# One register load for a group's expert weights, and key, turn, routing and ranks one or two slots later, in a sine-attention and mixture-of-experts kernel

## What is computed

```python
h = layernorm(x)
Q, K, V = (proj(h, W, b) for W, b in ((Wq, bq), (Wk, bk), (Wv, bv)))   # 16 heads of 8
attn = sin(30.0 * einsum('bhqd,bhkd->bhqk', Q, K) / sqrt(8))
x = x + einsum('bsd,ed->bse', heads_joined(einsum('bhqk,bhkd->bhqd', attn, V)), Wo) + bo

h = layernorm(x)
probs = sigmoid(einsum('bsh,eh->bse', h, Wr) + rb)                     # 8 experts
scores, idx = top_k(probs, 2)
cw = (one_hot(idx, 8) * scores[..., None]).sum(-2)
expert(h, Wg, Wu, Wd) = silu(h @ Wg.T) * (h @ Wu.T) @ Wd.T             # 128 -> 256 -> 128
x = x + expert(h, *shared) + sum_e cw[..., e:e+1] * expert(h, *routed[e])
```

## Time and profile before

| | |
|---|---|
| runs | 492.1, 491.87, 494.67 us; median 492.1 |
| profiled execution | 491.92 us, its span 490.0 us |
| mean granted TensorE clock | 0.981 |
| busy in the span | TensorE 427.6 us (87%), ScalarE 340.5 (70%), VectorE 292.0 (60%), GpSimd 238.6 (49%) |

### The profile page before, as it was taken

One profiled execution on the slowest core, in us unless ns is written; L12 is line 12 of the kernel. 1 busy time (PEld: TensorE's weight loads), 2 busy tenths in 40 slices (PEclk: granted clock), 3 DMA queues, 4 the chain that ended last, 5 costly groups with the idle time before them and its releaser, 6 DMA issues.

```text
span 490.0 us, 12316 instructions
## 1 busy us (share of the span) xinstructions
PE 427.6 (87%) x4432; PEld 224.0 (46%) x4432; DVE 292.0 (60%) x999; ACT 340.5 (70%) x470; POOL 238.6 (49%) x308
## 2 busy tenths in 40 slices
PE   2898899999978999899999998999999787978771
PEld 1321233323322445444554444444445776967761
DVE  6876685554723446578574666754654544547783
ACT  1668889878869986788688876777876453654540
POOL 5332450300565243228686854256856845567631
PEclk9999999999999999999999999999999978999996
DMA  5047589456046424962465349911122434431111
GB/s 166 2 132 207 117 245 328 91 159 166 18 128 178 98 56 123 185 121 70 132 189 127 70 135 191 167 55 55 50 61 56 104 98 111 113 98 44 50 50 32
DMA packets 82186, 56.05 MB, mean 114 GB/s; under 512 B 28752, under 2 KB 76496, under 8 KB 82128
## 3 DMA queue, kind: packets, MB, share of 16 engines
q1 hardware_dynamic: 77824, 47.74, 38.5%
q0 software_dynamic: 3584, 7.35, 5.6%
q10 hardware_dynamic: 720, 0.20, 0.2%
HBM read 22.62 MB, written 27.13 MB: 102 GB/s over the span
## 4 chain that ended last, share of the span: by engine, by line
PE 55%; issue 12%; DVE 11%; ACT 9%; another core or an unknown queue 3%; POOL 3%; DMA 3%; SPq 1%; ACTq 0%; DVEq 0%; POOLq 0%
PE o_ps L713 15%; PE score L700 8%; ACT attn L975 6%; PE tile_ps L840 4%; PE tile_ps L838 3%; PE tile_ps L839 3%; PE tile_ps L863 2%; DVE hid L1308 2%; ACT gate L996 2%; PE score L840 2%; DMA y_back<-in_wd 2%; PE r_ps L682 1%; PE score L838 1%; PE r_ps L669 1%
## 5 line engine op out<-in xcount | busy, mean ns | idle before, releaser
L975 ACT ACTIVATE attn<-score 128x1024 f32<-128x1024 f32 x256 | 248.5, 1025 | 31.3 <-PE score L700 26.2
L1532 POOL TENSOR_TENSOR hid_lo<-hid,hid_hi 128x256 f16<-128x256 f32 (+1 forms) x94 | 72.4, 771 | 157.8 <-DVE hid_hi L1316 125.2
L713 PE MATMUL o_ps<-attn,vals 128*32 128x512 f32 x1024 | 136.4, 604 | 0.8 <-ACT o_t L982 0.5
L700 PE MATMUL score<-queries,keys 64*128 64x512 f16 x512 | 83.3, 383 | 11.1 <-ACT attn L975 7.7
L1308 DVE SCALAR_TENSOR_TENSOR hid<-tile_ps,gate 128x256 f32<-128x256 f32 (+1 forms) x88 | 40.3, 458 | 55.6 <-ACT gate L996 44.7
L996 ACT ACTIVATE gate<-tile_ps 128x256 f32<-128x256 f32 (+1 forms) x88 | 36.4, 414 | 44.3 <-PE tile_ps L840 35.9
L838 PE MATMUL tile_ps<-xt,w_hi 128*128 128x128 f16 x244 | 43.9, 219 | 1.3 <-ACT y_sb L1008 0.7
L839 PE MATMUL tile_ps<-xt,w_hi 128*128 128x128 f16 x244 | 43.9, 219 | 0.8 <-issue 0.8
L840 PE MATMUL tile_ps<-xt,w_lo 128*128 128x128 f16 x244 | 43.9, 219 | 0.5 <-issue 0.5
L700 PEld LDWEIGHTS score<-queries,keys 64*128 64x128 f16 x512 | 18.5, 93 | 55.8 <-ACT attn L975 31.8
L863 PEld LDWEIGHTS tile_ps<-w_hi,hid_hi 128*128 128x128 f16 x152 | 14.7, 97 | 58.9 <-issue 53.2
(11 more groups left out here) (223 smaller groups left out, 993.6 us busy)
## 6 DMA issues: line engine op xcount, KB each, us to landing
q_four<-q_parts SPq DMA_DIRECT2D x14, 256.0 KB
queries<-q_four SPq DMA_DIRECT2D x14, 256.0 KB
k_four<-k_minus SPq DMA_DIRECT2D x14, 256.0 KB
keys<-k_four SPq DMA_DIRECT2D x14, 256.0 KB
y_sorted<-y_sb SPq DMA_DIRECT2D x52, 64.0 KB
x_sorted<-zeros SPq DMA_DIRECT2D x2, 1472.0 KB, 8.9
queries<-q_three SPq DMA_DIRECT2D x14, 192.0 KB
keys<-k_three SPq DMA_DIRECT2D x14, 192.0 KB
```

What stands on the lines that cost most here:

```text
L700: mm = pe.matmul(score[h][:, i, :], keys[b % 2][rows, 2 * j + h, kt * P:(kt + 1) * P], queries[b % 2][rows, 2 * j + h, :], start=True, sto ...
L713: mm = pe.matmul(o_ps[32 * i:32 * i + 32, :], vals[b % 2][:, kt, h:h + 32], attn[k % RING][:, i, :], start=(k == 0), stop=(k == UNITS - 1))
L975: act.activation(attn[k % RING][:, 2 * (u % 2):2 * (u % 2) + 2, :], score[u % 2][:, :, :], ACT.Sin, scale=SIN_SCALE).then_inc(sined, 1)
L1532: pool.tensor_tensor(cells(hid_lo, d), cells(hid, d), cells(hid_hi, d), ALU.subtract).then_inc(lo_by_pool, 1)
```

## The change

The planner's batch goes from 6 to 23, so each group has one look-up with all its offsets. They come at slots 123, 187, 251 and 276. The key projection of the next row goes from slot 8 to 9 with its scaling (10), split (high half 11, low half still 12, negated 14) and store (15). The second turn goes from 16 to 17, its copy to 18, routing to 20, logits and tanh to 21, top two to 22, choice to 23, ranks from 23 to 25, the placing of tokens to 26 to 28, the scatters to begin at 28. `shares` keeps its slot (31). The plan of jobs follows: shared tile (b, 3) goes ahead of the group's first expert tile, which moves to slot 125, 189 or 253; 113 jobs in all, 76 in the loop and 37 in the tail, the last slot 336. GpSimd's first scatter of a group gets a wait for the first transposing load of the group before.

```diff
-S_XT1, S_COPYX1, S_Q, S_SCALEQ, S_K, S_SCALEK, S_V = 1, 2, 3, 4, 8, 9, 11
-S_QHI, S_QLO, S_KHI, S_KLO, S_PLACEV, S_KNEG = 5, 6, 10, 12, 13, 13
-S_STOREQ, S_LOADQ, S_STOREK, S_LOADK = 7, 12, 14, 20
+S_XT1, S_COPYX1, S_Q, S_SCALEQ, S_K, S_SCALEK, S_V = 1, 2, 3, 4, 9, 10, 11
+S_QHI, S_QLO, S_KHI, S_KLO, S_PLACEV, S_KNEG = 5, 6, 11, 12, 13, 14
+S_STOREQ, S_LOADQ, S_STOREK, S_LOADK = 7, 12, 15, 20
 S_STATS1, S_AGGR1, S_POW1, S_APPLY1, S_ADDBO = 27, 28, 28, 29, 31
 S_COPYO, S_OUT, S_RES, S_STATS2, S_AGGR2, S_POW2, S_APPLY2, S_XHI, S_XLO = 3, 6, 7, 8, 9, 9, 11, 14, 15
-S_XT2, S_COPYX2, S_ROUTE, S_LOGIT, S_TANH, S_TOP, S_CHOOSE = 16, 17, 19, 20, 20, 21, 22
-S_PREFIX, S_DISPATCH, S_SCATTER = 23, 24, 27
+S_XT2, S_COPYX2, S_ROUTE, S_LOGIT, S_TANH, S_TOP, S_CHOOSE = 17, 18, 20, 21, 21, 22, 23
+S_PREFIX, S_DISPATCH, S_SCATTER = 25, 26, 28
...
-BATCH = 6
+BATCH = 23
...
-                    if last and s == S_DISPATCH + 7:
+                    if last and s == S_DISPATCH + 5:
                         shares(GROUP_OF[j])
...
                 if (row, t, c) == (0, 0, 0):
                     pool.wait_ge(places_ready, g + 1)
                     pool.wait_ge(cleared, 32)
+                    if g:
+                        n = LOADS.index((g - 1, 0, 2))
+                        pool.wait_ge(xt_loaded[n % XT], 16 * (n // XT + 1))
```

## The result

The kernel after took 495.39 us in the median of its runs, the kernel before 492.72 beside it; the ratio of the two is 1.0058, 95% interval 1.0034 to 1.0081. It is slower by 2.9 us where 6.5 us of gain were forecast, and outside the forecast range. The profiled execution took 495.56 us, its span 493.1.

What follows compares the result with a forecast made beforehand. TensorE was taken to bound the kernel, with ScalarE close behind. Savings of 4.15, 1.26, 1.57, 1.8 and 0.3 less costs of 1.84 and 0.74 gave -6.5 us, 491.92 to 485.4; range 483 to 488, 8 in 10 within 480.5 to 491.

Steps and rivals of the forecast that it cites:

- Part 3: Second turn, slot 16 to 17: 1.57 us of TensorE waits saved, 1.84 us paid for the copy and 0.74 for route.
- Part 1: Expert look-ups in TensorE's queue, 4 in place of 15: 4.15 us saved, the four long loads covered at 0 us.
- The slope of 15 ns per place: Register loads: three places took 0.777 us and six 0.822, so 17 more places give 1.08 us for 23.
- The bounds of 0.78 and 5.5: Load of 23 places: at least 0.78 us (a three-place load), at most 5.5 us (group 0's four loads added).
- Part 2: Key projection, slot 8 to 9: its waits for the residual in rows 4 to 6 go, 1.26 us saved.
- Copy and route: Later turn: copy between sines 18 and 19 costs 1.84 us in rows 3 to 7, route 0.74 in rows 1 and 2.
- The saving of 1.57: Second turn in rows 4 to 7: TensorE's waits for the packed row go, 1.57 us in all.
- Part 4: Ranks, slot 23 to 25: waits for the mask in rows 2, 4, 6 and 7 shrink, 1.8 us saved (1.0 to 2.1).
- Part 5: Tail: 37 jobs, not 38; one gate, one copy and one hand-over less save 0.3 us (0 to 1.0).
- the clock rival: Half-clock stretches in the tail go, some 4.5 us less, 481 us: chance 0.08; more of them, 488.5: chance 0.03.
- A long load: Register loads grow with their places, 4.9 to 5.7 us for 23, TensorE stands: 502 us at 5.3; chance 0.07.
- the waits come back: Savings on key, turn and ranks return as sine waits; only loads and tail gain: -1.9, 490.0 us; chance 0.17.

## Why the prediction was wrong

The forecast was right in what would vanish and wrong in what would come in its place. Two steps of its sum failed. Part 3 moved the logits and the tanh to slot 21 and put them at nothing, without a reason; they cost 5.5 us. Part 1 put the four long loads at "covered, 0 us"; the three in the loop left TensorE idle for 2.4 us, and the down matmul behind the one in the tail waited 0.98. With these in the forecast's own sum, -6.5 + 5.5 + 2.4 + 1.0 gives +2.4 (an estimate), and +2.9 was measured. What else was off cancels to within the noise. Point by point:

- **Part 1, the loads** ("All of these loads go: 2.85 + 1.30 = 4.15 us" and "17 more places give 1.08 us. I take that: covered, 0 us"). The first half came true in the trace, but it was not the fewer loads' alone: the tiles' later slot, which the forecast priced at nothing, takes the 2.85 us in the loop away with 15 loads too (0.9901 with the tiles alone), and together the two save them only once. The second half failed: 23 places take 2.1 to 2.3 us. The slope of 15 ns per place came from three and six places, which tell nothing of 23: this is the mis-sized term, 2.1 to 2.3 against 1.08. With a lead of some 1.5 us (from 173.32 to 175.77 less 0.91) that leaves 0.7 to 0.9 us three times. By runs: the long loads on top of the ranks part cost 0.9951 - 0.9913 = 0.0038, 1.9 us (from two different chips); by the pairs on the fast chip, 2.4 in the loop. The bounds of 0.78 and 5.5 held them, and a cost above 1.3 us had been named as already paid, but the value was taken from the near, cheap row. The Trainium skill ("Runtime: NRT & Kernel Launch", instruction fetch) has about 200 ns per register, for registers loaded from the chip's main memory; the loads of 23 from on-chip memory took 91 to 99 each. Its direction was right and half its size would have been the better guess.
- **Part 2, the key.** The waits went, 1.5 us in place. The measured 0.6 us holds the forecast of 1.26 only at the edge of its interval.
- **Part 3, the turn.** The waits at L739 went. Copy and route were forecast at 1.84 + 0.74 = 2.6 us. On the fast chip, from the kernel with the key alone to the kernel after, the pairs at slots 18 and 20 together grew by 0.40 in each of rows 1 and 2 (0.37 forecast), 0.73 in row 3 (0.24) and 0.45 in each of rows 4 to 7 (0.4), 3.3 us. That step held but for row 3. The saving of 1.57 was too small: beside the kernel with the turn back the pairs at slot 16 are 2.4 us shorter, and there the pairs behind them are only 2.4 longer. So the later turn is level, as the whole times say.
- **What was left out, and decides the sign.** Part 3 moved seven steps and priced three: turn, copy and route. The logits and tanh at slot 21 had no line in the sum. Part 4 even says of VectorE's choice that "one slot later" it "falls behind the hidden tile of slot 23", but did not ask the same of the logits, on which ScalarE waits with every sine behind it. Moved to an odd slot the logits stand behind the hidden tile of slot 21, and that is 5.5 us by the pairs and 5.7 by the ratios. With the tanh alone one slot later (0.9942) the kernel after is faster than before by 2.8 us.
- **Part 4, the ranks.** The waits at L762 went. The pairs at slot 22 of rows 2, 4, 6 and 7 shrank by 1.03, 0.70, 1.10 and 0.79 us from the kernel with the tiles alone to the one with the ranks part, more than the 1.8 forecast. But 0.9 came back at slot 24, and 1.5 at slot 30 of rows 2 and 4, where TensorE's down matmuls now wait 0.92 and 0.49 us for VectorE to read the tile before (the two lines of L863 at the end of the list of waits above). It is the logits' case again: the eight steps of `places` and `tile_experts`, two slots later, now stand ahead of that read in VectorE's queue (127.49 to 129.66 us in row 2 of the kernel with the ranks part), and the read begins at 129.57 where it began at 128.03 with the tiles alone. More came back in rows 5 and 7. The forecast priced only the choice of experts in VectorE's queue, and in the total nothing is left of the gain (0.9901 against 0.9913).
- **Part 5, the tail.** 119.4 to 115.6 us where 1.6 were forecast (1.30 of the loads and 0.3). Here single profiles mislead: the kernel before took 122.5 the second time, with as much of its tail at half clock (10.2 us) as the first time, and the kernel after had no half-clock stretch there. On the fast chip, where no tail had a half-clock stretch until TensorE's last 2 us, the kernel with the key alone took 101.1 us behind slot 254 and the kernel after 99.7: 1.4 less. So the forecast was near, and the rest of the 3.8 is the clock and scatter. A tail without the low clock is what the clock rival describes; that the change brought it about is not shown.
- **The rivals.** "A long load" had the right mechanism with 5.3 us for a load, which would have cost 16; "the waits come back" had the right sign for L700 (it was named: the forecast is wrong if they grow by 5 us; they grew by 8.0) but took it for savings returning. No case added a new wait to a sum of small savings. That was the rival missing.

The kernels, as ratios to the kernel before:

| kernel | ratio |
|---|---|
| tiles two slots later, short loads | 0.9901 |
| ranks part, short loads | 0.9913 |
| long loads alone | 0.9937 |
| ranks part, long loads | 0.9951 |
| ranks and key, long loads (the turn back) | 0.9941 |
| ranks and key, short loads (the turn back) | 0.9900 |
| kernel after (ranks, key, turn with tanh at 21, long loads) | 1.0058, 1.0040 on the fast chip |
| the same with short loads | 1.0018 |
| the same with tanh at 22, long loads | 0.9942 |
| the same with tanh at 22, short loads (mended) | 0.9901, 0.9867 on the fast chip |

The ledger that the runs give, in us against before: tiles two slots later -4.9, and with the ranks -4.3; long loads on top +1.9, so -2.4; key, turn and what follows it +5.3, so +2.9. Of the 5.3 the tanh is all. Each ratio has an interval of about 1 to 2 us either way, and they come from several chips; the pairs (tanh 5.5, loads 2.4) carry the account, the ratios agree with it.

## What to carry to other kernels

Ask of a blocking instruction how far the queue is ahead when it gets there; a wait just before it takes that lead away, and moving it two slots can be worth as much as removing it. When a group of steps moves by one slot, write down for each what now stands ahead of it in its own queue, the small ones first: a 0.18 us operation with a busy engine waiting for it cost more here (5.5 us) than the 4.15 us that the change was to save by the loads. And a change alone and the same change on top of another are two measurements.

## What the runs showed of the hardware

- The time of a register load from on-chip memory does not simply follow its number of places: from the table's start 6 took 0.82 to 1.03 us, 12 took 0.85 to 1.05, 16 took 1.24, 15 took 1.58 to 1.82, 24 took 1.62 to 1.80, 23 took 2.09 to 2.28. 24 places took 0.5 us less than 23, and 16 took 0.3 to 0.6 less than 15. Six places that begin at the seventh took 1.47 to 1.53 in the loop, six that begin at the thirteenth 0.81 to 0.93 in most cases (1.35 once), but 1.40 to 1.73 in all six cases right behind the turn. Whether it is the start, the end or the pieces in between was not tried.
- What such a load leaves idle is its time less the lead, that is the work already queued when it begins, and some 0.17 us more: 1.73 - 0.61 + 0.17 = 1.29 and 1.49 - 1.34 + 0.17 = 0.32 in the kernel before (1.29 and 0.31 in the trace), 2.28 - 1.54 + 0.17 = 0.91 in the kernel after (0.91).
- The same two kernels took 467.6 and 469.4 us on one chip and 489 to 495 in the median on the others. The median granted clock was 0.991 on the fast chip and 0.980 to 0.987 on the others. Each of the 14 profiles of the others has one to four stretches of 3.4 or 6.8 us at half clock (granted 0.50 or 0.51) while TensorE still works; the four of the fast chip have none until TensorE's last 2 us. That is worth 2 to 7 us (an estimate, half the length of these stretches), not 22. Row 3 and the tail hold most of the difference (the kernel after: 48.5 and 115.6 us on one, 43.1 and 99.7 on the fast one). In row 3 ScalarE stands idle and the profile names no engine of this core; first the kernel after on the first chip, then on the fast one:

```profile
147.54 2.85 ACT L975 ACTIVATE attn<-score 128x1024 f32<-128x1024 f32 x3 [3.61 <-remote]
...
159.85 2.86 ACT L975 ACTIVATE attn<-score 128x1024 f32<-128x1024 f32 x3 [2.47 <-remote]
```

```profile
145.54 1.94 ACT L975 ACTIVATE attn<-score 128x1024 f32<-128x1024 f32 x2 [1.06 <-PE score L700]
```

The first of these stalls is in before and after alike; the second came in some kernels and not in others, with no order by the edits. Its cause stays open, and it adds to the scatter of single profiles, which is why the ledger rests on ratios and on pairs outside row 3 where it could.
